# Hand-over from the first to the middle stage: where page copies, loads and first items' preparation stand in the queues

## The reference, cut

```python
x = x + attn(cond(x, ...adapter itok_B_1_7...), ...)      # first stage
# cond: x @ weight.T + bias + scale[id] * (x @ A[id].T) @ B[id].T
# attn: 32 heads of 16, 8 key/value heads, rotary, causal softmax over 128 tokens, dense
x = x + ffn(cond2(x, ...page table itok_Bx16_0_63, lengths...), ...)
# cond2 (middle stage): q, k, v = x @ Wq.T, x @ Wk.T, x @ Wv.T   (32 query, 8 key/value heads of 128)
#        RMS norm of q and k, rotary at the cached length
kc = k_cache[block_table].reshape(bsz, L, HK, D)          # 16 pages of 32 cached tokens per batch
vc = v_cache[block_table].reshape(bsz, L, HK, D)
#        softmax over 512 cached (masked) and 128 new keys, output projection
# ffn (last stage): x @ W.T + b plus a low-rank part whose rank the token chooses
```

## Time and profile before

| what | value |
|---|---|
| median of 3 runs | 1396.19 us (1395.92 to 1399.05) |
| the profiled execution | 1395.68 us, its span 1393.9 us |
| busy share of the span | PE 95%, weight loads 82%, DVE 77%, ACT 62%, POOL 47% |
| first stage | 0 to about 270 us, overlapping the middle stage from 234 us |
| middle stage | 64 items, 16.7 us for an item (cached keys' loads at 315.77, 332.51, 349.27) |
| page copies | 128, of 256 KB each |
| granted clock over the span | 0.985 |

### The profile page before, as it was taken

One profiled execution on the slowest core, in us unless ns is written; L12 is line 12 of the kernel. 1 busy time (PEld: TensorE's weight loads), 2 busy tenths in 40 slices (PEclk: granted clock), 3 DMA queues, 4 the chain that ended last, 5 costly groups with the idle time before them and its releaser, 6 DMA issues.

```text
span 1393.9 us, 26480 instructions
## 1 busy us (share of the span) xinstructions
PE 1328.4 (95%) x8088; PEld 1138.0 (82%) x8088; DVE 1068.3 (77%) x2951; ACT 861.1 (62%) x2499; POOL 655.9 (47%) x652
## 2 busy tenths in 40 slices
PE   4889997799999999999999999999999999999988
PEld 3666665588888888888888888888888888888877
DVE  3677866478888888888888888888888888888855
ACT  1567776466666676666666666676666667666631
POOL 1345546453545363536453654365345535453511
PEclk9799998999999999999999999999999999999999
DMA  7445444444121212121212122312212121213121
GB/s 259 146 149 159 158 153 140 134 114 114 31 66 37 80 32 62 31 77 32 61 32 77 31 61 41 82 40 51 71 38 61 32 76 32 61 31 73 28 74 61
DMA packets 193520, 107.59 MB, mean 77 GB/s; under 512 B 140897, under 2 KB 178274, under 8 KB 191970
## 3 DMA queue, kind: packets, MB, share of 16 engines
q1 hardware_dynamic: 192224, 105.38, 28.1%
q10 hardware_dynamic: 1154, 0.50, 0.1%
HBM read 101.66 MB, written 37.75 MB: 100 GB/s over the span
## 4 chain that ended last, share of the span: by engine, by line
PE 81%; SPq 10%; DVE 3%; issue 3%; DMA 2%; ACT 1%; POOL 0%; DVEq 0%; ACTq 0%; POOLq 0%
PE ps L1168 11%; PE ps L1170 11%; PE ps L1169 11%; PE ps L1219 10%; PE ps L1240 5%; PE ps L1233 5%; PE ps L1234 5%; SPq L79 5%; PE ps L1253 4%; SPq L80 4%; PE ps L1252 4%; PE ps L1259 4%; PE ps L1195 2%; PE ps L236 1%; PE ps L892 1%
## 5 line engine op out<-in xcount | busy, mean ns | idle before, releaser
L1365 ACT ACTIVATE b_pf<-b_sm,b_nb,b_rstd 128x640 f32<-128x640 f32 x256 | 235.2, 919 | 102.4 <-DVE b_nb L1470 102.2
L1371 ACT ACTIVATE b_p_h<-ps 128x640 fp32r<-128x640 f32 x256 | 180.3, 704 | 180.3 <-PE ps L1219 179.6
L1484 DVE TENSOR_TENSOR b_p_l<-ps,b_p_h 128x640 fp32r<-128x640 f32 x256 | 210.7, 823 | 82.9 <-ACT b_p_h L1371 75.8
L1463 DVE CUSTOM_DVE_ANT_0 b_sm<-ps,mask_row 128x640 f32<-128x640 f32 x256 | 209.3, 817 | 2.7 <-PE ps L1170 2.0
L1219 PE MATMUL ps<-ident,b_pf 128*128 128x128 f32 x1280 | 182.8, 274 | 10.0 <-DVE b_p_l L1484 8.0
L1479 DVE TENSOR_SCALAR b_pf<-b_pf,b_ri 128x640 f32<-128x640 f32 x256 | 159.0, 621 | 27.7 <-DVE b_ri L1476 0.5
L1168 PE MATMUL ps<-b_w_h,x1t_h 128*128 128x512 f32 (+1 forms) x512 | 179.2, 350 | 0.5 <-DVE b_qt_l L1451 0.5
L1219 PEld LDWEIGHTS ps<-ident,b_pf 128*128 128x128 f32 x1280 | 152.9, 141 | 29.6 <-issue 10.1
L1168 PE MATMUL ps<-b_kt_h,b_qt_h 128*128 128x320 f32 x512 | 174.6, 341 | 1.0 <-DVE b_mx L1463 1.0
L1169 PE MATMUL ps<-b_w_l,x1t_h 128*128 128x512 f32 (+1 forms) x512 | 173.4, 339 | 0.0
L1170 PE MATMUL ps<-b_w_h,x1t_l 128*128 128x512 f32 (+1 forms) x512 | 172.8, 337 | 0.0
(11 more groups left out here) (163 smaller groups left out, 3237.0 us busy)
## 6 DMA issues: line engine op xcount, KB each, us to landing
kv_of_batch<-in_kv SPq DMA_DIRECT2D x128, 256.0 KB
b_ck<-kv_of_batch SPq DMA_DIRECT2D x64, 256.0 KB, 3.6
b_cv<-kv_of_batch SPq DMA_DIRECT2D x256, 64.0 KB, 2.2
raw<-in_w SPq DMA_DIRECT2D x32, 384.0 KB, 5.4
raw<-in_wo SPq DMA_DIRECT2D x32, 256.0 KB, 3.6
a_xt<-in_xt SPq DMA_DIRECT2D x8, 256.0 KB, 5.1
a_xin<-in_x SPq DMA_DIRECT2D x8, 256.0 KB, 5.2
x<-a_x SPq DMA_DIRECT2D x8, 256.0 KB, 5.2
```

Source lines behind the costliest of these rows:

```text
L1365: act.activation(pf[:, h % 2], sm[:, h % 2], ACT.Exp, bias=nb[:, m.b % 2, h:h + 1], scale=rstd[:, m.b % 4, h:h + 1], accum_out=rs[:, m.b % ...
L1371: act.activation(p_h[:, :, h * P:(h + 1) * P], turned_row, ACT.Copy).then_inc(ph_sb, 1)
L1463: dve.tensor_tensor_reduce(sm[:, h % 2], score_row, mask_row[:, m.b], 1.0, MASKED, ALU.add, ALU.max, mx[:, k, h:h + 1]).then_inc(mx_sb, 1)
L1484: dve.tensor_tensor(p_l[:, :, cols], turned_row, p_h[:, :, cols], ALU.subtract).then_inc(pl_sb, 1)
```

## The change

Three kinds of edits, all in the hand-over:

1. SyncE's queue: `EARLY` 12 instead of 13; no copies in turn 7 (and so 96 instead of 117 in the first stage); `load_in` directly behind `store`, ahead of turn 7's wait; no wait for copies in turn 8. The 32 copies left go eight per item behind `rows(two)` for `two.b` = 2 to 5.
2. The low parts of head 0's weights: pieces c = 2 and 3 and the 1024 columns for keys and values leave GpSimd's turn 6 and go to VectorE's turn 7 (new functions `low_weights`, `low_kv_weights`). The first projection waits once for all four pieces.
3. Places: scores of item 0 ahead of `turn_probs(7, 7)`; `turn_next_k` ahead of `turn_probs(7, 5)`; on ScalarE `next_squares` ahead of `exponent(7, 5)` and `next_kv` ahead of `exponent(7, 6)`; on VectorE `next_products` ahead of `mask(7, 6)`; on GpSimd `next_queries` ahead of `normalize(7, 4)`.

```diff
--- before.py
+++ after.py
@@ -42,7 +42,7 @@
 QKV2 = (REP + 2) * HD
 SCALE2 = 1.0 / float(np.sqrt(HD))
 EPS = 1e-6
-EARLY = 13
+EARLY = 12
 LAST = B - 1
 MASKED = -1e30
 TWO_PI = (6.28125, 0.0019350051879882812, 3.019916050e-07)
@@ -186,19 +186,18 @@
             def slot(b):
                 if inside(b - 2):
                     store(b - 2)
+                if inside(b):
+                    load_in(b)
                 if b == LAST:
                     sp.wait_ge(gathered, 16 * EARLY * B)
                     cache_rows(Item(0, 0))
                 if b == LAST + 1:
-                    sp.wait_ge(gathered, 16 * EARLY * (B + 1))
                     cache_rows(Item(0, 1))
                     first_out_weights()
-                if inside(b):
-                    load_in(b)
                 if inside(b + 2) and b > -2:
                     load(b + 2)
-                if b > -2:
-                    for n in range((b + 1) * EARLY, min(b + 2, B + 1) * EARLY):
+                if -2 < b < LAST:
+                    for n in range((b + 1) * EARLY, (b + 2) * EARLY):
                         gather(sp, t, pages, kv_dram, gathered, n)
 
             slots(slot)
@@ -322,13 +321,13 @@
             def slot(b):
                 if inside(b - 1):
                     turn_probs(b - 1, 6)
+                if b == LAST + 1:
+                    pe.wait_ge(masked, 8 * B)
+                    next_scores(Item(0, 0), 0)
                 if inside(b + 1):
                     cond(b + 1)
                 if inside(b - 1):
                     turn_probs(b - 1, 7)
-                if b == LAST + 1:
-                    pe.wait_ge(masked, 8 * B)
-                    next_scores(Item(0, 0), 0)
                 if inside(b):
                     scores(b, 1)
                 if inside(b + 1):
@@ -366,12 +365,12 @@
                     turn_probs(b, 4)
                 if inside(b + 1):
                     scores(b + 1, 0)
+                if b == LAST:
+                    turn_next_k(Item(0, 0))
                 if inside(b):
                     turn_probs(b, 5)
                 if b == LAST:
                     project_next_q(Item(0, 1))
-                if b == LAST:
-                    turn_next_k(Item(0, 0))
                 if inside(b + 2):
                     low_rank(b + 2)
 
@@ -444,6 +443,8 @@
                     next_q_weights(0, 0)
                 if inside(b):
                     exponent(b, 4)
+                if b == LAST:
+                    next_squares(Item(0, 0))
                 if b == LAST - 1:
                     next_q_weights(0, 1)
                 if inside(b):
@@ -455,13 +456,11 @@
                 if b == LAST - 1:
                     next_q_weights(0, 2)
                 if b == LAST:
-                    next_squares(Item(0, 0))
+                    next_kv(Item(0, 0))
                 if inside(b):
                     exponent(b, 6)
                 if b == LAST - 1:
                     next_q_weights(0, 3)
-                if b == LAST:
-                    next_kv(Item(0, 0))
                 if inside(b):
                     probs_out(b, 3)
                 if b == LAST - 1:
@@ -567,17 +566,23 @@
                 dve.tensor_tensor(x1t_l[:, bass.ds(d, 1)].rearrange("p b k s -> p (b k s)"), ps[:, M0, :],
                                   x1t_h[:, bass.ds(d, 1)].rearrange("p b k s -> p (b k s)"), ALU.subtract).then_inc(xl_sb, 1)
 
-            next_products, next_values, next_queries, next_keys, next_maxima = ahead
+            next_products, next_values, next_queries, next_keys, next_maxima, next_low_weights, next_low_kv_weights = ahead
 
             def slot(b):
                 if inside(b):
                     mask(b, 2)
                     mask(b, 3)
                     invert(b, 0)
+                if b == LAST:
+                    next_low_weights(0, 2)
+                    next_low_weights(0, 3)
+                if inside(b):
                     mask(b, 4)
                     invert(b, 1)
                     invert(b, 2)
                     probs_out(b, 0)
+                if b == LAST:
+                    next_low_kv_weights(0)
                 if inside(b + 1):
                     q_out(b + 1)
                 if inside(b):
@@ -586,11 +591,11 @@
                     kv_out(b + 1)
                 if inside(b):
                     mask(b, 5)
+                if b == LAST:
+                    next_products(Item(0, 0))
+                if inside(b):
                     mask(b, 6)
                     probs_out(b, 2)
-                if b == LAST:
-                    next_products(Item(0, 0))
-                if inside(b):
                     invert(b, 4)
                 if inside(b + 1):
                     rope_sum(b + 1)
@@ -680,23 +685,16 @@
                     next_q_weights(0, range(0, 1))
                 if inside(b):
                     with_bias(b)
+                if b == LAST:
+                    next_queries(Item(0, 0))
                 if b == LAST - 1:
                     next_q_weights(0, range(1, 2))
                 if inside(b):
                     normalize(b, 4)
-                if b == LAST - 1:
-                    next_q_weights(0, range(2, 3))
-                if b == LAST:
-                    next_queries(Item(0, 0))
-                if inside(b):
                     normalize(b, 5)
                 if b == LAST:
                     next_rms(Item(0, 0))
                     next_keys(Item(0, 0))
-                if b == LAST - 1:
-                    next_q_weights(0, range(3, 4))
-                if b == LAST - 1:
-                    next_kv_weights(0)
                 if b == LAST:
                     next_cache_keys(Item(0, 0))
                 if b == LAST + 1:
@@ -1140,8 +1138,9 @@
                 if two:
                     rows(two)
                 if two and two.g == 0 and two.b in (2, 3, 4, 5):
-                    first = EARLY * (B + 1) + 3 * (two.b - 2)
-                    for n in range(first, min(first + 3, B * NPP)):
+                    count = (NPP - EARLY) * B // 4
+                    first = EARLY * B + count * (two.b - 2)
+                    for n in range(first, first + count):
                         gather(sp, t, pages, kv_dram, gathered, n)
                 if m and m.b == 3:
                     for c in range(KT):
@@ -1174,7 +1173,7 @@
                     pe.wait_ge(xl_sb, m.b + 1)
                 for k in range(KT):
                     if m.b == 0 and done is q_ps:
-                        pe.wait_ge(wql_sb, KT * m.g + k + 1)
+                        pe.wait_ge(wql_sb, KT * (m.g + 1) if m.g == 0 else KT * m.g + k + 1)
                     mm = three(ps[:, bank, 0:cols.stop - cols.start], (x1t_h[:, m.b, k], x1t_l[:, m.b, k]),
                                (w_h[:, k, cols], w_l[:, k, cols]), k == 0, k == KT - 1)
                 mm.then_inc(done, 1)
@@ -1533,7 +1532,18 @@
                 if last:
                     accumulate(last)
 
-            vector_first(dve, (rope_products, new_values, queries, new_keys, maxima))
+            def low_weights(g, c):
+
+                dve.wait_ge(wqh_sb, KT * g + c + 1)
+                dve.tensor_tensor(w_l[:, c, 0:D], raw[:, c, 0:D], w_h[:, c, 0:D], ALU.subtract).then_inc(wql_sb, 1)
+
+            def low_kv_weights(g):
+
+                dve.wait_ge(wkvh_sb, g + 1)
+                cols = slice(D, D + kv_width(g))
+                dve.tensor_tensor(w_l[:, :, cols], raw[:, :, cols], w_h[:, :, cols], ALU.subtract).then_inc(wkvl_sb, 1)
+
+            vector_first(dve, (rope_products, new_values, queries, new_keys, maxima, low_weights, low_kv_weights))
             h_rest, choose, rows_dve = dve_ffn
             slots(dve, slot)
             h_rest(dve, 0)
```

More of the change, by code:

```diff
@@ L588, in slot @@
                     mask(b, 5)
-                    mask(b, 6)
-                    probs_out(b, 2)
                 if b == LAST:
@@ L593, in slot @@
                 if inside(b):
+                    mask(b, 6)
+                    probs_out(b, 2)
                     invert(b, 4)
```

## The result

The changed kernel is slower by 0.3%, not faster: its median is 1401.68 us (1397.23 to 1402.50, 8 runs) beside 1396.83 us (1395.03 to 1399.05) for the kernel before, a ratio of 1.003 [1.002, 1.004]. The profiled execution took 1402.3 us, its span is 1400.4 us, the granted clock over it 0.984. The forecast was 1387.4 us in a range of 1382 to 1392.

The account below looks back on a forecast made before the run. SyncE's lagging queue and waits on other engines were taken to leave TensorE idle 18.6 of 67 us in the hand-over. 3.7 + 1.3 + 4.1 + 1.4 - 0.7 - 1.0 = 8.8 us took 1396.19 to 1387.4 us, range 1382 to 1392.

Parts of the forecast that it names:

- The four terms of the hand-over: Gains: 3.7 us up to b_ra, 1.3 half-clock work behind, 4.1 at item 1's values, 1.4 half-clock work behind.
- the clock's loss: Hand-over: several stops of 1 to 2.3 us might lower the clock once more; 1.0 us lost (0 to 3).
- item 3: Hand-over: earlier xin load and 12 copies a turn bring b_ra's transposes 3.7 us ahead, plus 1.3 us of half-clock work.
- The weights' own move: Hand-over projections: 2.9 us gained at the first, 2.3 us lost at the second, 0.6 us ahead.
- The rest of the 3.7 us: Hand-over, up to b_ra: GpSimd's 6.09 us wait for xin and TensorE's 3.00 us go, beside the weights' 0.6.
- item 5: Middle stage: eight copies 15.2 us plus own transfers 2.2 make 17.4 us in a 16.7 us item; 0.7 us lost.
- the slack of 7 us: Middle stage: the in-between items' lateness of 4 to 5 us stays under a slack of 7 us.
- The prediction's own sign: Middle stage: ScalarE waiting over 3 us at item 6 would make the prediction wrong; SyncE's last wait should end near 350.
- the third rival: Middle stage: copies bind; at 2.25 us each all gain is eaten, at 2.5 us about 1405 us; chance 0.07.
- The bound "0 to 3 us" for item 6: Middle stage: range of the 0.7 us loss at item 6, values landing 2.2 us (1.9 to 3.5) after the last start.
- The wait ahead of item 6: Middle stage: waiting for the last copy, SyncE sends item 6's keys at 359.4, values 1.4 us late; 0.7 us lost.
- 1.7 us of losses in the middle stage and by the clock: Deducted from the gain: 0.7 us for late values at item 6 and 1.0 us for the clock in the hand-over.

Follow-up runs that it names:

- e7: e4 with the six moved calls put back to their old places: hand-over 87.42 us, median 1390.55 us, ratio 0.9955.
- e8: e4 with the load of xin back behind turn 7's wait and item 0's rows: hand-over 84.35 us, median 1387.49 us, ratio 0.9931.
- e1: Kernel after with the copies and the wait of the kernel before, moved work kept: hand-over 94.76 us, median 1397.22 us, ratio 1.0011.
- e3: Kernel after with each item's values issued ahead of its keys: items 3 to 8 92.49 us, median 1394.70 us, ratio 0.9993.
- e5: Kernel after with head 0's keys loaded as 128 rows of 2 KB, wrong numbers: items 3 to 8 88.63 us, median 1391.00 us, ratio 0.996.
- e9: Kernel after with the last 16 copies on their own semaphore, item 6 waiting for 112: median 1402.08 us, ratio 1.0036.
- e10: e3 with the last 16 copies on their own semaphore, item 6 waiting for 112: median 1395.49 us, ratio 0.999.
- e4: Kernel after with the 32 copies spread: 5 in turn 7, 3 in turn 8, 5 behind items 2 to 5, 4 at 6: 1387.60 us, ratio 0.9942.
- e11: e4 with the low part of the 1024 key and value columns on GpSimd in turn 7, not VectorE: median 1386.22 us, ratio 0.9925.
- e6: e4 with the low parts of the weights back on GpSimd in turn 6: hand-over 84.96 us, median 1386.75 us, ratio 0.9932.
- e2: Kernel before with only the new copy numbers and distribution and no wait in turn 8: hand-over 90.35 us, median 1410.29 us, ratio 1.0116.

## Why the prediction was wrong

**Right, with its sizes: the hand-over.** Of the earlier trace rows, 238.09 became 235.35 (235.2 forecast), 239.94 became 239.39 (239.3), 250.25 became 246.55 (246.55). The transposes of 281.98 came at 272.24, 9.7 us ahead (9.1). The first projection started at 231.41 (231.2), and TensorE's wait ahead of the second was 1.96 us (2.3), as the kernel after shows:

```profile
231.41 0.77 PE L1167 MATMUL ps<-b_w_h,x1t_h 128*128 128x512 f32 x1 [0.31 <-DVE b_w_l L1538]
...
237.91 0.36 PE L1167 MATMUL ps<-b_w_h,x1t_h 128*128 128x256 f32 x1 [1.96 <-issue]
```

The four terms of the hand-over sum to 10.5 us (3.7 + 1.3 + 4.1 + 1.4), 9.5 with the clock's loss; 10.3 to 10.6 were measured. Some luck is in this agreement, as the next point shows.

**Right in the sum, wrong in the causes: item 3.** The weights' own move gives 0.7 us (0.6 forecast). The rest of the 3.7 us was put under the load of `xin`, with `next_products` moved up beside it; two of the other places were taken at nothing, or up to 1 us lost, and three have no price at all. But the six places together are worth 3.1 us (e7), and the load's new order is worth nothing (e8). What frees `xin` is that a turn has 12 copies instead of 13: with 13 the load of `xin` leaves at 238.40, although it stands ahead of turn 7's wait (e1), with 12 at 227.59.

**Wrong: item 5, "the item's own five transfers 2.2" us.** This is the step that failed. That figure is of issues with few copies ahead of them. Behind eight copies the five take 6.3 us (311.92 to 318.22), because of the form of the keys' load and because the values stand behind it (e3, e5). The 17.4 us a turn became 21.6, the overrun of 0.7 us an item became 4.9, and the slack of 7 us that the prediction leaned on was used up by item 4. The lost time, 15.9 us, parts by e5 into about 11 for the hold and 5 for item 6, where the transfers stand behind copies and weight loads. The parts do not simply add: with the values first (e3), where the queue's turn stays 0.8 us longer than in e5, only 7.1 us come back, and 8.8 are left, most of them at item 6. The prediction's own sign for this came true: ScalarE waits 7.45 us at item 6, where over 3 us was to make it wrong, and the queue's last wait ends at 360.27 instead of near 350.

**Right outcome, wrong cause: the third rival.** It said that the copies bind the middle stage, decided by a copy above 1.94 us, and got a chance of 0.07. The copies cost 1.8 to 1.9 us, no more than forecast. The price was in what stands behind them in the same queue, for which the trace of before had no case: there, at most three copies stand ahead of an item's rows without a wait between. Its longest issue of values, 1.708 us against a median of 0.43, was in the view and was not asked about; it stands near 706 us, where no copy is ahead, so it is not the same case. The bound "0 to 3 us" for item 6 rested on landing times of 1.9 to 3.5 us, taken from a queue with at most three copies an item; the longest landing of values after is 6.1 us.

**The wait ahead of item 6** was priced as the thing that decides (1.4 us late). e9 and e10 show that it decides nothing: taking it away changes items 3 to 8 by 0.1 and 0.6 us.

**The clock** was costed at 1.0 us and in the hand-over rose to 1.00 from 250 on. It fell in the middle instead, where TensorE now stands (one stretch of the kernel before, then two of the kernel after):

```profile
340.00:357.00 17.00, 17.00 (x105) 15.16 (x104) 13.85 (x34) 10.68 (x31) 6.64 (x7) 1.00 0.48 140
...
340.00:357.00 17.00, 13.93 (x73) 12.29 (x72) 10.05 (x23) 9.21 (x26) 5.47 (x5) 0.80 0.44 130
357.00:374.00 17.00, 10.88 (x50) 9.30 (x49) 7.77 (x22) 6.20 (x20) 3.93 (x4) 0.80 0.54 147
```

**e4 near 1387.4 us is no proof of the prediction.** Its sum had 1.7 us of losses in the middle stage and by the clock that e4 does not have there, a hand-over term that came from other causes, and no term for the slower stretch at the end (last section).

## What to carry over

A transfer queue has a turn time, like an engine: before work is put into it, add up all that it issues in one turn at the durations of a loaded queue, and compare with the turn of the engines; where the trace has no loaded case, say so and leave the bound open on that side. The longest single issue of values of the kernel before (1.71 us, 1.3 above the median) over four turns would have given about 5 us, an estimate from those rows and still a third of the 15.9 lost. A gain ahead of a stage is kept only if the work that made room for it is laid where the queue has free time (e4, 5 an item), not where it just fits on average. Inside a turn, what an engine waits for goes ahead of the transfer that holds the queue (e3). Two chains that hide each other (here transfers and engine work) gave 4.4 us for the first alone, 0 for the second alone and 10.6 for both: parts of such a change must not be priced one by one.

## What the runs showed of the hardware

**An issue can be held by the transfer ahead of it.** The issue of 64 KB behind a transfer of 2048 rows of 128 B takes 4.43 and 4.13 us with eight copies of 256 KB issued right ahead, and 0.43 in the median. After five copies and four loads of weights, four such issues take 5.34 us (e4). Behind 128 rows of 2 KB, four such issues take 1.85 us together with the same copies ahead. The Trainium skill ("DMA: Bandwidth & Descriptors", "Specifications") gives 512 B as the smallest size that runs at line rate. The two shapes of the keys' load lie on either side of it, though no run here measured the rate by itself, and that the rate is what holds the queue is not shown.

**VectorE stands while GpSimd subtracts.** An operation on 4 columns took 2.21 us instead of 0.17 beside GpSimd's 1024 columns and ended with them (e11), as the 1.43 us of the earlier trace rows had shown in small.

**The clock after the same stop is not always the same.** In the last items of the middle stage all kernels have a stop of TensorE of 2.1 us. The stretch behind it, first in the kernel before, then in the kernel after:

```profile
1319.30:1335.00 15.70, 12.74 (x72) 10.71 (x72) 11.42 (x28) 8.20 (x16) 3.56 (x3) 1.00 0.51 168
...
1324.30:1340.00 15.70, 14.29 (x72) 11.96 (x72) 10.05 (x25) 6.63 (x14) 3.52 (x3) 0.89 0.50 168
```

The 72 matmuls of the stretch take 12.74 and 14.29 us, at 1.00 and 0.89. From this stop to TensorE's next stop of over 1 us (1.74 us), the profiled execution takes 15.2 us in the kernel before, e1, e3, e5 and e6, and 16.8 us in the kernel after, e2, e4 and e7 to e11. So it is one of two lengths, and not the kernel's speed elsewhere, that adds 1.6 us there; it is as large as the differences between e4, e6 and e8, which is a reason to compare those by the hand-over and not by the median. What decides it stays open.
